# The gates of the second expert network: the first chunk's ahead of the products, the others' between the steps

## What is computed

```python
def _L1_ffn_ref(x, w_gate, w_g, w_u, w_d):
    B, S, D, M, E, K = (2, 256, 128, 176, 8, 2)
    scores = x @ w_gate
    topk_scores, topk_idx = jax.lax.top_k(scores, K)
    topk_probs = jax.nn.softmax(topk_scores, axis=-1)
    gating = jnp.sum(jax.nn.one_hot(topk_idx, E, dtype=topk_probs.dtype) * topk_probs[..., None], axis=-2)
    hidden = jax.nn.silu(jnp.einsum('bsd,edm->ebsm', x, w_g)) * jnp.einsum('bsd,edm->ebsm', x, w_u)
    expert_out = jnp.einsum('ebsm,emd->ebsd', hidden, w_d)
    y = jnp.einsum('bse,ebsd->bsd', gating, expert_out)
    return y
```

## Time and profile before

| | us |
|---|---|
| median of 3 runs (3241.26 to 3244.34) | 3242.34 |
| the profiled execution | 3239.29 |
| its span, from first to last instruction | 3237.5 |
| first such network: first cast on VectorE (L636), first product on TensorE (L571) | 1053.78, 1071.62 |
| second such network: the same two | 3010.27, 3028.11 |
| first output product of the first network (L584) | 1098.02 |

### The profile page before, as it was taken

One profiled execution on the slowest core, in us unless ns is written; L12 is line 12 of the kernel. 1 busy time (PEld: TensorE's weight loads), 2 busy tenths in 40 slices (PEclk: granted clock), 3 DMA queues, 4 the chain that ended last, 5 costly groups with the idle time before them and its releaser, 6 DMA issues. The chain is left out here.

```text
span 3237.5 us, 65499 instructions
## 1 busy us (share of the span) xinstructions
PE 2699.6 (83%) x20208; PEld 1143.7 (35%) x20208; DVE 2756.8 (85%) x4594; ACT 2436.5 (75%) x2621; POOL 1936.7 (60%) x1284
## 2 busy tenths in 40 slices
PE   3994899998898897488888888888888888883899
PEld 2772333334676454222222222222222222222455
DVE  4996888885898666699999999999999999986665
ACT  3983577777696454389999999999999999992454
POOL 3220122222222454099999999999999999993454
PEclk9997899999798899699999999999999999996799
DMA  3002110010000000200000000000000000000000
GB/s 96 1 0 87 30 30 28 28 29 11 2 0 0 1 1 0 89 12 16 11 12 14 11 14 12 11 15 11 11 15 11 13 13 11 15 1 1 4 11 13
DMA packets 52651, 56.00 MB, mean 17 GB/s; under 512 B 12144, under 2 KB 34672, under 8 KB 52560
## 3 DMA queue, kind: packets, MB, share of 16 engines
q1 hardware_dynamic: 52560, 54.87, 5.7%
HBM read 39.37 MB, written 14.68 MB: 17 GB/s over the span
## 5 line engine op out<-in xcount | busy, mean ns | idle before, releaser
L1463 POOL TENSOR_TENSOR a_sg<-a_sg,a_shifted 128x1664 f32<-128x1664 f32 x256 | 955.6, 3733 | 21.4
L1660 DVE TENSOR_REDUCE a_mx<-a_pm 128x1 f32<-128x1024 f32 x512 | 619.9, 1211 | 20.3 <-PE a_pm L1502 20.3
L1669 DVE TENSOR_SCALAR a_sg<-a_pa 128x1024 int32<-128x1024 int32 x512 | 619.9, 1211 | 4.9 <-PE a_pa L1502 4.6
L1582 ACT ACTIVATE a_pt<-a_pb 128x1024 f32<-128x1024 f32 x512 | 524.3, 1024 | 108.1 <-PE a_pb L1502 108.1
L1519 PE MATMUL a_po<-a_pt,a_Vh 128*32 128x512 f32 x2048 | 539.8, 606 | 2.2 <-ACT a_sg L1601 2.2
L1519 PE MATMUL a_po<-a_sg,a_Vh 128*32 128x512 f32 x2048 | 539.8, 606 | 0.0
L1460 POOL TENSOR_SCALAR a_shifted<-a_sg,a_parh 128x1664 f32<-128x1664 f32 x256 | 470.8, 1839 | 100.5 <-DVE a_sg L1669 63.0
L1597 ACT ACTIVATE a_sg<-a_sg,a_parh 128x2048 f32<-128x2048 f32 x256 | 511.8, 1999 | 0.0
L1601 ACT ACTIVATE a_sg<-a_sg 128x2048 f32<-128x2048 f32 x256 | 489.9, 1914 | 0.0
L1502 PE MATMUL a_pm<-all_K,all_Q 96*128 96x512 bf16 x1024 | 315.8, 391 | 151.4 <-DVE a_mx L1660 125.1
L1281 ACT ACTIVATE a_pt<-a_ring 128x1024 f32<-128x1024 f32 (+2 forms) x384 | 313.7, 846 | 166.0 <-PE a_ring L1208 162.7
(11 more groups left out here) (237 smaller groups left out, 5399.3 us busy)
## 6 DMA issues: line engine op xcount, KB each, us to landing
all_Q<-q_parts SPq DMA_DIRECT2D x256, 48.0 KB
all_K<-k_parts SPq DMA_DIRECT2D x256, 48.0 KB
k_parts<-p_parts SPq DMA_DIRECT2D x16, 384.0 KB, 2.5
all_Q<-a_rows SPq DMA_DIRECT2D x384, 2.0 KB
q_parts<-p_parts SPq DMA_DIRECT2D x16, 192.0 KB, 2.4
q_parts<-p_parts SPq DMA_DIRECT2D x8, 384.0 KB, 2.6
all_Q<-q_parts SPq DMA_DIRECT2D x64, 32.0 KB
all_K<-k_parts SPq DMA_DIRECT2D x64, 32.0 KB
```

The source lines that it names most:

```text
L1463: nc.gpsimd.tensor_tensor(buf[:, :, 0:CUT], buf[:, :, 0:CUT], shifted[:], ALU.mult)\
L1582: nc.scalar.activation(pt[(j - LT) % 4][:, i, :], pb[:], ACT.Exp, scale=SC)\
L1660: nc.vector.tensor_reduce(mx[:, (j // PER) % 2, t:t + 1], pm[:], AX.X, ALU.max)\
L1669: nc.vector.tensor_scalar(sg[(j - LS) % 4][:, i, :].bitcast(I32), pa[:].bitcast(I32), SIGN_OFF, None, ALU.bitwise_and).then_inc(abs_done, 1)
```

## The change

The gates are now worked out in two parts, `PARTS`: the 4 tiles of the first chunk, and the other 28. The 23 operations of a part are cut into pieces (`step` 0 to 3 and 6 to 8). All pieces of the first part run in the head. The pieces of the second part are issued on VectorE behind steps 0 to 3 and 6 to 8 of chunk 0. The transposes of the gates go to a bank of their own (`pst`), those of the first chunk ahead of the products, those of chunks 1 to 7 behind steps (0,9), (1,0), (1,2), (1,4), (1,6), (1,8) and (1,10), with the copy to `gateT` behind silu of the same step on ScalarE. The exponential of the second part stands behind silu of step (0,5). TensorE waits for a chunk's gates only ahead of its first product into `psm`.

```diff
@@ -492,11 +492,15 @@
         psu = m.ps("psu", [P, 2, CH])
         psm = m.ps("psm", [P, 2, CH])
         psy = m.ps("psy", [P, 4, D])
-        ident_ready, chain, e2, saved = (m.sem(x) for x in ("identb", "chain", "e2", "saved"))
-        cleared, gate_ready, turned, gate_out = (m.sem(x) for x in ("cleared", "gate", "turned", "gateout"))
+        pst = m.ps("pst", [P, CH])
+        ident_ready, chain, exp_out, saved = (m.sem(x) for x in ("identb", "chain", "expout", "saved"))
+        cleared, turned, gate_out = (m.sem(x) for x in ("cleared", "turned", "gateout"))
         g_done, u_done, m_done, silu_done, su_done, hid_done, high_done, low_done, y_done, added = (
             m.sem(x) for x in ("gd", "ud", "md", "silu", "sud", "hidd", "high", "low", "yd", "added"))
         EARLY = 4
+        PARTS = (slice(0, NT // NCH), slice(NT // NCH, NT))
+        GATE_OPS, GAP_OPS = 23, 12
+        TURNS = {(0, 9): 1, (1, 0): 2, (1, 2): 3, (1, 4): 4, (1, 6): 5, (1, 8): 6, (1, 10): 7}
 
         def chunks(eng, body):
 
@@ -547,16 +551,18 @@
             def _(pe):
                 pe.wait_ge(weights_in, FFN1_LOADS)
 
-                pe.wait_ge(gate_ready, 1)
                 pe.wait_ge(ident_ready, 1)
-                for c in range(NCH):
-                    if c >= 2:
-                        pe.wait_ge(gate_out, c - 1)
-                    out = psm[:, c % 2, :].bitcast(BF16)
+
+                def turn_gates(c):
+                    pe.wait_ge(chain, GATE_OPS if c == 0 else 2 * GATE_OPS)
+                    if c:
+                        pe.wait_ge(gate_out, c)
+                    out = pst[:].bitcast(BF16)
                     for q in range(4):
                         last = nc.tensor.transpose(out[0:96, q * P:(q + 1) * P], gate3[:, 4 * c + q, :], identb[:])
                     last.then_inc(turned, 1)
-                pe.wait_ge(gate_out, NCH)
+
+                turn_gates(0)
 
                 def step(c, p, k):
                     b = bank(p, k)
@@ -571,6 +577,8 @@
                         nc.tensor.matmul(out[:, b, :], high, xh, start=True, stop=False)
                         nc.tensor.matmul(out[:, b, :], high, xl, start=False, stop=False)
                         nc.tensor.matmul(out[:, b, :], low, xh, start=False, stop=True).then_inc(done, 1)
+                    if k == 0:
+                        pe.wait_ge(gate_out, c + 1 if isinstance(c, int) else NCH)
                     nc.tensor.matmul(psm[:, b, :], sel[:, k, :], gateT[:, bass.ds(c * CH, CH)],
                                      start=True, stop=True).then_inc(m_done, 1)
 
@@ -590,6 +598,8 @@
                 def chunk(c, p):
                     for k in range(KT1):
                         step(c, p, k)
+                        if isinstance(c, int) and (c, k) in TURNS:
+                            turn_gates(TURNS[c, k])
                         if k == EARLY - 1 and not (isinstance(c, int) and c == 0):
                             output(c - 1, 1 - p)
 
@@ -598,12 +608,17 @@
 
             @block.scalar
             def _(act):
-                act.wait_ge(e2, 1)
-                nc.scalar.activation(pr[:, 1, :], pr[:, 0, :], ACT.Exp).then_inc(e2, 1)
-                for c in range(NCH):
+                def exp_gap(part):
+                    act.wait_ge(chain, part * GATE_OPS + GAP_OPS)
+                    nc.scalar.activation(pr[:, 1, PARTS[part]], pr[:, 0, PARTS[part]], ACT.Exp).then_inc(exp_out, 1)
+
+                def gates_out(c):
                     act.wait_ge(turned, c + 1)
-                    nc.scalar.activation(gateT[:, c * CH:(c + 1) * CH], psm[:, c % 2, :].bitcast(BF16)[0:96, 0:CH],
+                    nc.scalar.activation(gateT[:, c * CH:(c + 1) * CH], pst[:].bitcast(BF16)[0:96, 0:CH],
                                          ACT.Copy).then_inc(gate_out, 1)
+
+                exp_gap(0)
+                gates_out(0)
 
                 def silu(c, p, k):
                     b = bank(p, k)
@@ -623,6 +638,10 @@
                 def chunk(c, p):
                     for k in range(KT1):
                         silu(c, p, k)
+                        if isinstance(c, int) and (c, k) == (0, 5):
+                            exp_gap(1)
+                        if isinstance(c, int) and (c, k) in TURNS:
+                            gates_out(TURNS[c, k])
                         if k:
                             high(c, p, k - 1)
                         elif not (isinstance(c, int) and c == 0):
@@ -635,29 +654,55 @@
             def _(dve):
                 nc.vector.tensor_copy(identb[:], ident[:]).then_inc(ident_ready, 1)
                 link = Chain(dve, chain)
-                first_argmax(link, nc, one1, score, top, pref, eq, rank, E1)
-
-                link(nc.vector.scalar_tensor_tensor(rest[:], one1[:], -3.0e38, score[:], ALU.mult, ALU.add))
-                first_argmax(link, nc, one2, rest, top2, pref, eq, rank, E1)
-
-
-                nc.vector.tensor_tensor(pr[:, 0, :], top2[:], top[:], ALU.subtract).then_inc(e2, 1)
-                dve.wait_ge(e2, 2)
-                link(nc.vector.tensor_scalar(pr[:, 0, :], pr[:, 1, :], 2.0 * WSCALE, 2.0 * WSCALE, ALU.mult, ALU.add))
-                link(nc.vector.reciprocal(pr[:, 2, :], pr[:, 0, :]))
-                link(nc.vector.tensor_tensor(pr[:, 3, :], pr[:, 2, :], pr[:, 1, :], ALU.mult))
-                link(nc.vector.tensor_tensor(gate[:], one1[:], pr[:, 2, :].unsqueeze(2).broadcast_to([P, NT, E1]),
-                                             ALU.mult))
-                link(nc.vector.tensor_tensor(eq[:], one2[:], pr[:, 3, :].unsqueeze(2).broadcast_to([P, NT, E1]),
-                                             ALU.mult))
-                link(nc.vector.tensor_tensor(gate[:], gate[:], eq[:], ALU.add))
-
-                dve.wait_ge(cleared, 1)
-                link(nc.vector.tensor_copy(gate3[:, :, 0:E1], gate[:]))
-                link(nc.vector.tensor_tensor(gate[:], gate[:], gate3[:, :, 0:E1], ALU.subtract))
-                link(nc.vector.tensor_copy(gate3[:, :, 32:32 + E1], gate[:]))
-                link(nc.vector.tensor_tensor(gate[:], gate[:], gate3[:, :, 32:32 + E1], ALU.subtract))
-                nc.vector.tensor_copy(gate3[:, :, 64:64 + E1], gate[:]).then_inc(gate_ready, 1)
+
+                def gates(part, step):
+
+                    t = PARTS[part]
+                    n = t.stop - t.start
+
+                    def wide(column):
+                        return column.unsqueeze(2).broadcast_to([P, n, E1])
+
+                    def first(onehot, source, best, half):
+                        if half == 0:
+                            link(nc.vector.tensor_reduce(best[:, t], source[:, t], AX.X, ALU.max))
+                            link(nc.vector.tensor_tensor(eq[:, t], source[:, t], wide(best[:, t]), ALU.is_equal))
+                            link(nc.vector.tensor_tensor(pref[:, t], eq[:, t],
+                                                         rank[:].unsqueeze(1).broadcast_to([P, n, E1]), ALU.mult))
+                        else:
+                            link(nc.vector.tensor_reduce(eq[:, t, 0], pref[:, t], AX.X, ALU.max))
+                            link(nc.vector.tensor_tensor(onehot[:, t], pref[:, t], wide(eq[:, t, 0]), ALU.is_equal))
+
+                    if step < 2:
+                        first(one1, score, top, step)
+                    if step == 1:
+                        link(nc.vector.scalar_tensor_tensor(rest[:, t], one1[:, t], -3.0e38, score[:, t],
+                                                            ALU.mult, ALU.add))
+                    if step in (2, 3):
+                        first(one2, rest, top2, step - 2)
+                    if step == 3:
+                        link(nc.vector.tensor_tensor(pr[:, 0, t], top2[:, t], top[:, t], ALU.subtract))
+                    if step == 6:
+                        dve.wait_ge(exp_out, part + 1)
+                        link(nc.vector.tensor_scalar(pr[:, 0, t], pr[:, 1, t], 2.0 * WSCALE, 2.0 * WSCALE,
+                                                     ALU.mult, ALU.add))
+                        link(nc.vector.reciprocal(pr[:, 2, t], pr[:, 0, t]))
+                        link(nc.vector.tensor_tensor(pr[:, 3, t], pr[:, 2, t], pr[:, 1, t], ALU.mult))
+                        link(nc.vector.tensor_tensor(gate[:, t], one1[:, t], wide(pr[:, 2, t]), ALU.mult))
+                    if step == 7:
+                        link(nc.vector.tensor_tensor(eq[:, t], one2[:, t], wide(pr[:, 3, t]), ALU.mult))
+                        link(nc.vector.tensor_tensor(gate[:, t], gate[:, t], eq[:, t], ALU.add))
+                        if part == 0:
+                            dve.wait_ge(cleared, 1)
+                        link(nc.vector.tensor_copy(gate3[:, t, 0:E1], gate[:, t]))
+                        link(nc.vector.tensor_tensor(gate[:, t], gate[:, t], gate3[:, t, 0:E1], ALU.subtract))
+                    if step == 8:
```

(8 more changed lines are left out.)

## The result

| | before | changed | forecast |
|---|---|---|---|
| median, us (6 runs each) | 3241.48 | 3253.61 | 3254.0 |
| lowest to highest | 3240.27 to 3244.34 | 3250.28 to 3254.70 | 3243 to 3261 |
| ratio to before, 95% interval | | 1.0035, 1.0025 to 1.0045 | 1.0036 |
| profiled execution, span | 3239.29, 3237.5 | 3254.70, 3253.0 | |

The changed kernel is slower by 12.1 us of 3241. Run a second time beside other runs of before, it gave 3252.12 against 3242.72, 9.4 us more, ratio 1.0035 (1.0021 to 1.0049).

What follows compares the result with a forecast made beforehand. Bound: a serial gate chain in each second network's head, then VectorE in chunk 0. Terms -9.3 + 7.5 + 4.7 + 1.1 + 2.4, less 0.5, give +5.9 a network, twice +11.8: 3254 us, range 3243 to 3261.

Steps and rivals of the forecast that it cites:

- The head: Chain ahead of each second expert network's first product: working out 4 tiles instead of 32 saves 9.3 us a network.
- Gate operations on VectorE: Chunk 0: 23 operations for the other 28 tiles between steps; 8.8 us, of which 7.5 a network stay on the path.
- Holding: Chunk 0: GpSimd's subtraction holds one VectorE gate operation in each of five steps, 0.93 us each, +4.7 a network.
- The exponential: Second exponential on ScalarE between silu 5 and high 4: two table loads delay su 6, +1.1 us a network.
- Turns: Seven groups of transposes on TensorE with ScalarE copies, between steps of chunks 0 and 1: +2.4 us a network.
- the pair of turns: Two turns two steps apart: the first costs 0.78 us, the second about 0.1, so up to 0.9 a pair.
- Clock: Rival: TensorE's granted clock falls back between pieces in chunk 0, up to 2.5 us a network more, 3259; chance 0.13.
- main case: The forecast itself: all terms as summed, 3254 us, own range 3249 to 3258; chance 0.60.
- the 0.5: Taken off each network's sum, since a longer lower clock behind the first product would hide step 1's gates too.

Runs made afterwards that it cites:

- the kernel with holding alone: Changed kernel without turns behind steps and with Silu for the second exponential, GpSimd's subtraction in chunk 0 kept: 3247.18 us, ratio to before 1.0017.
- the kernel before with the memset: Kernel before with GpSimd's subtraction of chunk 0 replaced by a memset of the low part: 3242.11 us, ratio to before 1.0001.
- the head alone: Changed kernel without the second part's gate operations, second exponential and turns behind steps; all chunks use chunk 0's turned gates: 3221.92 us, ratio to before 0.9938.
- v1: Changed kernel with eight tiles in the head, first later piece behind step (0,0), the others and exponential behind (1,3), turns moved: 3228.58 us, ratio to before 0.9955.
- v2: v1 with the turns of chunks 3 to 7 in the loop, behind step 3 of the chunk before: 3231.11 us, ratio to before 0.9965.

## Why the prediction was right

*The head.* -9.3 forecast; the first product moved by 9.4, and the network gained 10.0, since the lower clock behind the first product was also shorter. Right; the size of the last part was not foreseen, and it depends on when the clock rises.

*Gate operations on VectorE.* +7.5 forecast, +7.45 by the medians, 6.6 by the traces, of which 0.35 is the cast beside the memset. The reading that VectorE has no idle time in chunk 0 but ahead of su 1, and that step 0's piece fits there, held: VectorE's idle time ahead of su 1 is 0.27 us in the changed kernel. Too dear by about 1, as said above: the prediction counted the 0.10 between VectorE's operations as waits for its own results, and the pieces, which do not need those results, fill them.

*Holding.* +4.7 forecast. The five operations that were named, the third of steps 1, 2 and 3, the last of step 6 and the cast of step 7, are the five that are long, 1.39, 1.39, 1.18, 1.25 and 1.27, and step 8 has none. They are 1.00, 1.00, 0.99, 0.86 and 1.00 longer than unheld, where 0.93 each was forecast. 4.7 by the traces of the kernel with holding alone, 5.2 with the clock's part.

*The exponential.* +1.1 forecast; 1.2 by the medians, 1.0 by the traces, 1.39 us idle ahead of su 6.

*Turns.* +2.4 forecast; 1.2 by the medians, 1.6 by the traces: mis-sized. The step that failed is the pair of turns: I charged four of them in chunk 1 with 1.5, and they cost 0.8. VectorE's waits for silu behind these four are 0.54, 0.40, 0.54 and 0.54 us; without turns it waits 0.18 us every second step and 0.26 at the last. A turn there costs 0.2 us in the mean (0.8 for four), where a pair was charged up to 0.9.

*Clock.* Forecast as a rival at 0.13 beside a main case in which nothing falls, and with 0.5 taken off for it. In all four networks of the changed kernel's two profiles it fell, so the rival's mechanism was there in the main case. Against the 228.1 without falls it cost 0.2 to 0.5 in the first networks, where it was low while VectorE was the bound, and 1.7 to 1.9 in the second, where it was low again behind step 8; in one network of another run it cost 3.7. The main case was wrong on this, by 1.5 us a network with the 0.5, and small only in the mean.

*What I did not have: the last output products.* Between the profiled executions the difference is 15.5 us, not 12.1. Of it 4.1 are at the end of the two networks and 1.8 outside of them. VectorE's last additions wait for TensorE's last output products, before and in the changed kernel:

```profile
1277.67 0.89 DVE L681 SCALAR_TENSOR_TENSOR all_X<-f_psy,all_X 128x128 f32<-128x128 f32 x4 [9.53 <-PE f_psy L586]
```

```profile
1285.09 0.88 DVE L726 SCALAR_TENSOR_TENSOR all_X<-f_psy,all_X 128x128 f32<-128x128 f32 x4 [12.14 <-PE f_psy L594]
```

9.53 and 12.14 us. In the changed kernel's profile the clock was 0.51 from 1273.5 to 1280.3, from the pause of 3.30 us ahead of the output products until well into them. The change is not needed for it: the kernel before with the memset has it too in one of its two networks,

```profile
1280.85 0.88 DVE L684 SCALAR_TENSOR_TENSOR all_X<-f_psy,all_X 128x128 f32<-128x128 f32 x4 [11.16 <-PE f_psy L589]
```

and the second profile of the changed kernel has 9.53 in its first network. Over the 28 networks of the profiles the wait is 9.53 where the clock did not fall in it, 10.9 to 11.2 where it was low for 3.4 us and 12.1 to 12.3 where it was low for 6.8. It adds up to 5.4 us to one execution and none to another, and is probably part of why the six runs of a kernel spread over 4 us. Whether the change makes it more frequent is open: the wait is the longer one in 15 of the 18 networks that have gate operations between the steps of chunk 0, and in 1 of the 6 of the kernel before, with and without the memset, and the head alone.

Right in sum, then, and partly by luck. Without the difference of the last waits, a network of the changed kernel is 4.7 us longer than before (229.1 against 224.4), where 5.9 was forecast: the head -10.1 and not -9.3, the gate operations with what held them 11.3 and not 12.2, the exponential 1.0 and not 1.1, the turns 1.6 and not 2.4, the clock +1.0 and not -0.5 (4.8, with rounding). The medians gave 6.05 in the first comparison and 4.7 in the second; over all 11 executions of the changed kernel and all 81 of before the means, 3252.9 and 3242.1, give 5.4. That the first median came within 0.4 us of the forecast is luck: terms that were off by 0.8, 0.9, 0.8 and 1.5 us a network cancelled in part. What lies between 4.7 and 5.4 may be the last waits or noise; no run tells.

## What to carry to other kernels

A chain of short operations ahead of a stage is worth its length, but where it is moved counts more than that it is moved: between steps whose bound is the same engine it costs nearly its full time again, and beside a GpSimd operation that reads SBUF a two-input operation on VectorE costs up to that operation's whole length more. Look for the place where the engine waits for another one (here 6 us behind step 3, while TensorE makes the output products), and put the work there in one run, function-table switches with it. And before a profile's difference is explained, look at the clock throughout the stage and at its ends: one network can be 2.8 us off in a place that the change does not touch, and 3.7 in a place that it does.

## What the runs showed of the hardware

A tensor_tensor of 28 elements a partition took 1.18 us beside a GpSimd subtraction and 0.188 beside a GpSimd memset; a cast of 224 took 1.27 beside the subtraction, 0.62 beside the memset and 0.27 alone. A table load took 1.28 us, and the operation behind it began 1.29 to 1.30 after the load's start. Four transposes with their copy cost nothing that shows behind steps (1,4) to (1,9) of v1, and 0.25 us a chunk beside the output products in v2. TensorE's granted clock also fell to 0.50 in stretches in which the engine had work in every step: in the changed kernel at 1075.6 us, 1.2 us after a pause of 1.99 us, the longest since its rise.
